# Two graph layers in one kernel: the order of transfers, splittings and matmuls in the first four groups

## What is computed

```python
# layer 0, per graph; 8 heads of 48
q, k, v = x @ wq + bq, x @ wk + bk, x @ wv + bv
scores  = q k^T * 48**-0.5 + adj
ctx     = softmax(scores) @ v
x1      = rmsnorm(x + ctx @ wo + bo) * alpha1 + gamma1
ff      = silu(x1 @ w1 + b1) @ w2 + b2                  # 384 -> 1536 -> 384
x2      = rmsnorm(x1 + ff) * alpha2 + gamma2
x       = layernorm(x + x2)
# layer 1: attention with 12 heads, then layernorm(x + attention(x))
```

## Time and profile before

| | |
|---|---|
| runs | 1919.75, 1922.04, 1927.74 us |
| profiled execution | 1929.19 us, of which 1927.4 us are the span from the first to the last instruction |
| PE busy | 1885.5 us (98%) in 23481 matmuls |
| DVE, ACT, GpSimd busy | 1279.8 (66%), 1084.8 (56%), 496.6 us (26%) |
| DMA | 213.49 MB, 40.2% of 16 engines' span |
| PE in slices of a fortieth | 7 tenths in the first, 8 in the second, 9 or more in all others but the last (7) |
| mean granted TensorE clock | 0.993 of full |

### The profile page before, as it was taken

One profiled execution on the slowest core, in us unless ns is written; L12 is line 12 of the kernel. 1 busy time (PEld: TensorE's weight loads), 2 busy tenths in 40 slices (PEclk: granted clock), 3 DMA queues, 4 the chain that ended last, 5 costly groups with the idle time before them and its releaser, 6 DMA issues.

```text
span 1927.4 us, 60766 instructions
## 1 busy us (share of the span) xinstructions
PE 1885.5 (98%) x23481; PEld 1853.4 (96%) x23481; DVE 1279.8 (66%) x2507; ACT 1084.8 (56%) x2366; POOL 496.6 (26%) x615
## 2 busy tenths in 40 slices
PE   7899999999999999999999999999999999999997
PEld 7899999999999999999999999999999999999997
DVE  6566666666666666666666666654577777777775
ACT  4365555655555654556555565544466666666665
POOL 0121113121122121221211312112134444444443
PEclk9899999999999999999999999999999999999999
DMA  7544444444444434444444344445222333333232
GB/s 190 155 113 108 118 133 109 126 119 109 128 117 118 126 110 128 122 112 123 118 111 136 109 124 116 112 119 122 60 79 84 87 89 90 90 90 90 83 89 68
DMA packets 268686, 213.49 MB, mean 111 GB/s; under 512 B 142816, under 2 KB 251104, under 8 KB 268640
## 3 DMA queue, kind: packets, MB, share of 16 engines
q1 hardware_dynamic: 268640, 212.85, 40.2%
HBM read 120.33 MB, written 79.69 MB: 104 GB/s over the span
## 4 chain that ended last, share of the span: by engine, by line
PE 90%; DMA 2%; SPq 2%; DVE 2%; ACT 1%; issue 1%; POOL 0%; ACTq 0%; POOLq 0%; DVEq 0%
PE a_bank L446 30%; PE a_banks L446 29%; PE b_bank L1444 15%; PE b_banks L1444 5%; PE b_banks L1496 2%; PE a_banks L519 2%; PE b_bank L1515 2%; PE b_banks L1488 2%; PE a_bank L499 2%; SPq L263 1%; DMA xt_raw<-in_xT 0%; PE a_bank L578 0%; DMA ctx_turned<-a_work 0%; DMA a_work<-ctx_turned 0%; DMA xt_raw<-x2T 0%
## 5 line engine op out<-in xcount | busy, mean ns | idle before, releaser
L446 PE MATMUL a_bank<-a_x1t_hi,a_w_hi 128*128 128x256 f32 x1152 | 328.2, 285 | 4.1 <-DVE a_x1t_lo L939 4.1
L446 PE MATMUL a_bank<-a_x1t_lo,a_w_hi 128*128 128x256 f32 x1152 | 325.1, 282 | 0.0
L446 PE MATMUL a_bank<-a_x1t_hi,a_w_lo 128*128 128x256 f32 x1152 | 324.9, 282 | 0.0
L757 ACT ACTIVATE a_work<-a_bank,a_b 128x256 f32<-128x256 f32 x384 | 160.3, 469 | 201.5 <-PE a_bank L446 201.1
L446 PE MATMUL a_banks<-a_w_hi,a_hid_hi 128*128 128x384 f32 x768 | 258.7, 337 | 2.1 <-DVE a_hid_lo L954 2.1
L954 DVE TENSOR_TENSOR a_hid_lo<-a_work,a_hid_hi 128x512 fp32r<-128x512 f32 x192 | 130.7, 694 | 192.8 <-ACT a_hid_hi L762 192.8
L446 PE MATMUL a_banks<-a_w_lo,a_hid_hi 128*128 128x384 f32 x768 | 258.7, 337 | 0.0
L446 PE MATMUL a_banks<-a_w_hi,a_hid_lo 128*128 128x384 f32 x768 | 258.6, 337 | 0.0
L446 PEld LDWEIGHTS a_bank<-a_x1t_hi,a_w_hi 128*128 128x128 f32 x1152 | 218.8, 190 | 6.4 <-DVE a_x1t_lo L939 4.4
L446 PEld LDWEIGHTS a_bank<-a_x1t_lo,a_w_hi 128*128 128x128 f32 x1152 | 221.3, 192 | 0.0
L446 PEld LDWEIGHTS a_bank<-a_x1t_hi,a_w_lo 128*128 128x128 f32 x1152 | 218.0, 189 | 0.0
(11 more groups left out here) (177 smaller groups left out, 5628.2 us busy)
## 6 DMA issues: line engine op xcount, KB each, us to landing
a_work<-in_x SPq DMA_DIRECT2D x64, 384.0 KB, 3.2
p_turned<-a_work SPq DMA_DIRECT2D x256, 64.0 KB, 2.2
a_work<-p_turned SPq DMA_DIRECT2D x32, 512.0 KB, 3.2
xt_raw<-in_xT SPq DMA_DIRECT2D x32, 384.0 KB, 3.9
ctx_turned<-a_work SPq DMA_DIRECT2D x256, 48.0 KB, 1.7
a_work<-ctx_turned SPq DMA_DIRECT2D x32, 384.0 KB, 3.4
x_turned<-a_work SPq DMA_DIRECT2D x256, 48.0 KB, 1.7
a_work<-x_turned SPq DMA_DIRECT2D x32, 384.0 KB, 3.8
```

Source lines behind the costliest of these rows:

```text
L446: r = pe.matmul(out, lhs[a], rhs[b], start=first and n == 0, stop=last and n == 2)
L757: r = act.activation(silu[:, p % 2, s * GROUP:(s + 1) * GROUP], A[p % 3][:, s * GROUP:(s + 1) * GROUP], ACT.Silu, bias=b1[:, m:m + 1])
```

## The change

All in the first layer, in the four `begin` lists and in what they call with group 0 or 1:
- SP: P(0)'s eight stores and the load follow the adjacency of group 1, ahead of w1's second slice. x of group 3 is loaded right behind the constants. w1's third slice moves behind P(1)'s transfers. The stores of x1(0) stand ahead of `load_x(1)`, of `swap_v(2)` and of w2's second half; between its stores and its load stands the first tile of ctx(1), behind the load the second tile, the adjacency of group 3 and ctx(1)'s load.
- Buffers: the blocks of x1(0) are written to `x_bo` in place of `blocks`. `turn_x1(0)` no longer waits for ctx(0)'s stores, `turn_ctx(1)` waits for these in place of x1(0)'s stores, and `load_x(1)` waits for x1(0)'s stores.
- PE: part 0 of `qk(2)` goes ahead of `pv(0)` in place of 30 filling matmuls; the other parts and V follow. 32 filling matmuls stand ahead of `attn_out(0)`; the 45 behind it and the 64 ahead of the feed-forward part go. In the feed-forward part of group 0 `attn_out(1)` moves ahead of `ffn1(0, 3)` and `ffn2(0, 1)`.
- ACT and DVE: the lists follow: `split_x(3)`, `take_pt(1)` and the squares come ahead of w1's third slice and w2; DVE takes ctx(1) ahead of `scale_x1(0)`, with a new wait on the squares; K of group 3, P(2)'s transposition and the low part of x1(0) come ahead of `w1_low(2)`, `w2_low` and V of group 3; x1(1) is made two parts of the hidden layer earlier.

The diff, without the lines that only surround it:

```diff
@@ -46,7 +46,7 @@
...
 N_TURNED = TILES * P // 32
-FILL_FIRST, FILL_LAST, FILL_QK, FILL_OUT = 64, 40, 80, (22, 16)
+FILL_FIRST, FILL_LAST, FILL_QK, FILL_OUT = 32, 40, 80, (22, 16)
@@ -218,6 +218,10 @@
...
+        def x1_blocks(g):
+            return x_bo if isinstance(g, int) and g == 0 else blocks
@@ -233,6 +237,8 @@
...
             def load_x(g):
+                if isinstance(g, int) and g == 1:
+                    sp.wait_ge(x1_stored, 16 * N_TURNED)
                 wait(sp, y1_done, TILES * g)
@@ -273,7 +279,7 @@
...
                 sp.wait_ge(x1_turned, TILES * g + t + 1)
-                store_blocks(blocks, scratch["x1"], t, x1_stored)
+                store_blocks(x1_blocks(g), scratch["x1"], t, x1_stored)
@@ -380,14 +386,14 @@
...
                 load_adj(1)
+                for t in range(TILES):
+                    store_p(0, t)
+                load_pt(0)
                 sp.wait_ge(w_lo, WV + 1)
                 load_w1(1)
-                for t in range(TILES):
-                    store_p(0, t)
-                load_pt(0)
-                load_w1(2)
                 load_x(0)
                 load_consts()
+                load_xt(3)
@@ -398,21 +404,21 @@
...
                 load_pt(1)
-                load_xt(3)
+                load_w1(2)
                 load_w2(range(0, 6))
+                for t in range(TILES):
+                    store_x1(0, t)
+                store_ctx(1, 0)
+                load_x1t(0)
+                store_ctx(1, 1)
+                load_adj(3)
+                load_ctxt(1)
                 load_x(1)
...
                     swap_v(2, t)
-                for t in range(TILES):
-                    store_x1(0, t)
-                load_x1t(0)
                 sp.wait_ge(w1_lo, 2)
                 load_w2(range(6, FC))
-                for t in range(TILES):
-                    store_ctx(1, t)
-                load_adj(3)
-                load_ctxt(1)
                 for t in range(TILES):
@@ -448,9 +454,9 @@
...
-            def qk(g):
+            def qk(g, parts=range(3)):
                 pe.wait_ge(xt_lo, g + 1)
-                for u in range(3):
+                for u in parts:
                     if isinstance(g, int) and g == 0:
@@ -582,9 +588,13 @@
...
                 ffn2(f, 0, new)
+                early = back and isinstance(f, int) and f == 0
+                if early:
+                    for t in range(TILES):
+                        attn_out(f + 1, t, new)
                 ffn1(f, 3, new, back)
                 ffn2(f, 1)
-                if back:
+                if back and not early:
                     for t in range(TILES):
@@ -640,23 +650,21 @@
...
                 scores(1)
-                fill("wq", 30)
+                qk(2, (0,))
                 wait_for_pv(0, True)
...
                     pv(0, t)
-                qkv(2)
+                qk(2, (1, 2))
+                for t in range(TILES):
+                    values(2, t)
+                fill("wq", FILL_FIRST)
                 for t in range(TILES):
                     attn_out(0, t, True)
-                pe.wait_ge(ctx_done, 2)
-                fill("wq", 45)
                 wait_for_pv(1, True)
...
                 qkv(3)
-                pe.wait_ge(ctx_done, TILES * 2)
-                pe.wait_ge(w1_lo, 1)
-                fill("w1", FILL_FIRST)
                 feed_forward(0, True, True)
@@ -855,32 +863,31 @@
...
                     take_q(2, u)
+                split_x(3)
+                ctxt_high(0)
+                for t in range(TILES):
+                    take_pt(1, t)
+                for t in range(TILES):
+                    square(x1, y1_done, ssq1, sq1_done, t + 1, t, ctxt[:, t, :])
+                for t in range(TILES):
+                    keep_v(2, t)
                 w1_high(2)
-                ctxt_high(0)
-                split_x(3)
-                for t in range(TILES):
-                    square(x1, y1_done, ssq1, sq1_done, t + 1, t, ctxt[:, t, :])
-                for t in range(TILES):
-                    take_pt(1, t)
                 w2_high(range(0, 6))
-                for t in range(TILES):
-                    keep_v(2, t)
                 for t in range(TILES):
...
                 act.wait_ge(const_loaded, 16 * N_CONST)
-                for p in range(2):
-                    hidden(0, p)
+                hidden(0, 0)
+                ctxt_high(1)
+                hidden(0, 1)
                 w2_high(range(6, FC))
-                ctxt_high(1)
-                for p in (2, 3):
-                    hidden(0, p)
+                hidden(0, 2)
                 for t in range(TILES):
                     square(x1, y1_done, ssq1, sq1_done, TILES + t + 1, t, ctxt[:, t, :])
-                for p in (4, 5):
+                for p in range(3, FP):
                     hidden(0, p)
@@ -993,7 +1000,9 @@
...
                 dve.wait_ge(ctx_done, 2 * (g + 1))
-                if t == 0:
+                if t == 0 and isinstance(g, int) and g == 1:
+                    dve.wait_ge(ctx_stored, 16 * N_TURNED)
+                elif t == 0:
                     wait(dve, x1_stored, 16 * N_TURNED * g)
@@ -1016,9 +1025,9 @@
...
                 dve.wait_ge(x1_done, TILES * g + t + 1)
-                if t == 0:
+                if t == 0 and not (isinstance(g, int) and g == 0):
                     dve.wait_ge(ctx_stored, 16 * N_TURNED * (g + 1))
-                dve.transpose(blocks[:, t, :], x1[:, t, :]).then_inc(x1_turned, 1)
+                dve.transpose(x1_blocks(g)[:, t, :], x1[:, t, :]).then_inc(x1_turned, 1)
@@ -1191,48 +1200,50 @@
...
                     turn_p(1, t)
+                take_k(2)
+                for t in range(TILES):
+                    take_v(2, t)
+                split_x(3)
                 w1_low(1)
-                take_k(2)
-                for t in range(TILES):
-                    take_v(2, t)
                 turned_low(ctx_t, turned_raw, ctxt_hi, ctxt_lo, 1)
-                split_x(3)
-                w1_low(2)
                 for t in range(TILES):
...
+                dve.wait_ge(sq1_done, TILES)
+                for t in range(TILES):
+                    take_ctx(1, t)
                 dve.wait_ge(const_loaded, 16 * N_CONST)
...
-                for t in range(TILES):
-                    take_ctx(1, t)
                 for t in range(TILES):
...
                     shift(2, t)
+                take_k(3)
+                for t in range(TILES):
+                    turn_p(2, t)
+                turned_low(x1_t, x1t_raw(0), x1t_hi, x1t_lo, 1)
+                w1_low(2)
                 w2_low(range(0, 6))
                 for t in range(TILES):
-                    turn_p(2, t)
-                take_k(3)
-                for t in range(TILES):
                     take_v(3, t)
-                turned_low(x1_t, x1t_raw(0), x1t_hi, x1t_lo, 1)
-                for p in range(2):
+                hidden_low(0, 0)
+                turned_low(ctx_t, turned_raw, ctxt_hi, ctxt_lo, 2)
+                hidden_low(0, 1)
+                w2_low(range(6, FC))
+                hidden_low(0, 2)
+                for t in range(TILES):
+                    take_y1(1, t)
+                scale_x1(1)
+                hidden_low(0, 3)
+                for t in range(TILES):
+                    turn_x1(1, t)
+                for p in (4, 5):
                     hidden_low(0, p)
-                w2_low(range(6, FC))
-                turned_low(ctx_t, turned_raw, ctxt_hi, ctxt_lo, 2)
-                for p in (2, 3):
-                    hidden_low(0, p)
-                for t in range(TILES):
-                    take_y1(1, t)
-                hidden_low(0, 4)
-                scale_x1(1)
-                for t in range(TILES):
-                    turn_x1(1, t)
-                hidden_low(0, 5)
                 for t in range(TILES):
```

More of the change, by code:

```diff
@@ L382, in begin @@
                 load_adj(1)
-                sp.wait_ge(w_lo, WV + 1)
-                load_w1(1)
                 for t in range(TILES):
@@ L387, in begin @@
                 load_pt(0)
-                load_w1(2)
+                sp.wait_ge(w_lo, WV + 1)
+                load_w1(1)
                 load_x(0)
                 load_consts()
+                load_xt(3)
                 for t in range(TILES):
@@ L857, in begin @@
                     take_q(2, u)
-                w1_high(2)
+                split_x(3)
                 ctxt_high(0)
-                split_x(3)
+                for t in range(TILES):
+                    take_pt(1, t)
                 for t in range(TILES):
@@ L864, in begin @@
                 for t in range(TILES):
-                    take_pt(1, t)
+                    keep_v(2, t)
+                w1_high(2)
                 w2_high(range(0, 6))
-                for t in range(TILES):
-                    keep_v(2, t)
                 for t in range(TILES):
@@ L1193, in begin @@
                     turn_p(1, t)
-                w1_low(1)
```

(27 more changed lines are left out.)

## The result

The changed kernel takes **1907.12 us** (median of 6 runs, 1903.66 to 1913.06); the kernel before, run beside it, 1922.22 us (6 runs, 1919.75 to 1927.74). The ratio is 0.9919 with a 95% interval of 0.9906 to 0.9932: 15.1 us less, where 13.3 were forecast. The profiled execution took 1906.83 us, its span 1905.0, against 1927.4 before.

What follows compares the result with a forecast made beforehand. PE's own work was taken to set the middle, so time won in the first four groups ends the kernel earlier. The sum of -13.3 on the profiled 1929.19 gives 1915.9; that execution lies 7.15 above the median, so 1908.7 us, range 1903.0 to 1914.5.

Steps and rivals of the forecast that it cites:

- pv(0): P times V of group 0 on PE: start at 38.95 in place of 40.68, 1.7 us earlier.
- pv(1): P times V of group 1 on PE: start at 59.75 in place of 68.35, 8.6 us earlier.
- x1: Group 0's x1: turn_x1 at 64.4, load at 70.8, low part ready and ffn1 starting at 76.3, 15.3 us earlier.
- The first ffn2: Group 0's first ffn2: start at 84.5 against 97.77, 13.3 us earlier, behind 4.7 us of DVE's low parts.
- From the first ffn2 22.09 us without a hole: First ffn2 to the end of group 0: PE had worked 22.09 us there without a hole.
- I keep it at its old price: Stall of 2.17 us at scores(3), explained by no semaphore, counted as unchanged.
- stalls vanish: Rival: scores(3) unbroken and the loop's first round losing its 3.5 us, -15.5 to -19.0, 1905 us; chance 0.15.
- The clock: New holes before attn_out(0) and ffn1 risk descents of 1.6 to 2.1 us each, falling into slack, 2.1 before ffn2.
- clock on the path: Rival: three ffn1 at reduced clock take 10.7 us, ending at 87.0; 2.5 us lost, 1911.2 us; chance 0.13.
- Late landings: Rival: stores of P, ctx and x1 meet other transfers, 5.4 us lost, -7.9, 1914.1 us; chance 0.14.
- slower: Rival: a stall like the 2.17 us at scores(g) in each of 27 loop rounds, 1967 us; chance 0.03.

Runs made afterwards that it cites:

- p_behind: Changed kernel with P(0)'s stores and load behind w1's second slice again; one profiled execution took 1917.61 us.
- xt_late: Changed kernel with x of group 3 loaded behind P(1) again, ahead of w1's third slice; one profiled execution took 1915.79 us.
- x_later: Changed kernel with only load_x(1) moved, behind V(2)'s swaps and w2's second half; one profiled execution took 1909.39 us.
- after_again: The changed kernel once more, unchanged; one profiled execution took 1916.04 us.
- lows_first: Changed kernel with w1_low(2) and three of the first six w2_low ahead of x1's low part on DVE; one profiled execution took 1904.30 us.
- after: The changed kernel itself, as profiled in the first pair with the kernel before; that execution took 1906.83 us.
- one_buffer: Changed kernel with x1(0)'s blocks back in the buffer of ctx's blocks and the two old waits; one profiled execution took 1915.32 us.
- q_behind: Changed kernel with 30 fillings ahead of pv(0) again and all of qk(2) behind it; one profiled execution took 1921.76 us.
- attn_late: Changed kernel with attn_out(1) back behind ffn2(0, 1); one profiled execution took 1908.59 us.
- combo: Changed kernel with the edits of x_later and lows_first, plus 56 fillings for 32 before attn_out(0) and 30 before ffn1; ratio 0.9935 to the kernel before.

## Why the prediction was right

Total, sign and most of the way were right. Two terms of the sum were not, +2.2 at the first ffn2 and -2.6 behind pv(2); that they cancelled is luck.

- **pv(0)**: 1.7 forecast; the profiled pair has 2.7 and p_behind 2.3 to 3.0. The step counted SP's issue time of one slice only; from p_behind to the change the stores come 2.2 earlier, and a load behind the slice took longer (3.6 to 6.5 us against 3.4 to 3.8). pv(1) comes earlier by the same amount.
- **pv(1)**: 59.75 forecast, 59.60 seen, but for another reason. ACT was done at 58.9; PE was still in `attn_out(0)`, 5.85 us at a granted 0.52, after a hole of 3.16. So the clock took back what the earlier P had given. That the two cancelled is chance too. xt_late bears out the cause of the 8.6: x of group 3.
- **x1**: `turn_x1` 64.37 (64.4), load issued at 71.42 (70.8), ffn1 76.95 (76.3). The four issues of ctx(1) took what they should; x1's eight stores took 4.52 in place of 3.90.
- **The first ffn2**: in the profiled execution this step failed by 2.2 us. "1.75 + 6 x 0.49 = 4.7" was DVE's work taken from a stretch without GpSimd; beside GpSimd's additions it was 6.2 (76.81 to 83.02, w1's slice included). 0.6 came from the later ffn1. Where the additions fell elsewhere, as in x_later, ffn1 to ffn2 took 8.17, and the forecast had 8.2.
- **"From the first ffn2 22.09 us without a hole"**: 86.74 to 108.94 is 22.20. Right.
- **"I keep it at its old price" (scores(3))**: wrong. From pv(2) to ffn1 of group 1 it was 2.76 us (108.94 to 111.70) in place of 5.37 (119.86 to 125.23). Only 1.0 of the 2.6 is the stall that is gone; 1.6 are x1(1), which the forecast had made earlier without giving it a term, since the old stall hid the wait for it. The 2.6 make up for what the first ffn2 had lost: 11.0 + 2.6 = 13.6, and at pv(3) 13.5 were measured. The rival "stalls vanish" had this half right, and wrong in the loop's first round, 41.2 to 44.7 in all kernels.
- **The clock**: 7.74 us for the three ffn1 at 0.82, inside the slack, since DVE was late anyway. In after_again they took 8.54 at 0.73 and ffn2 came straight behind: there the rival "clock on the path" held, but at some 0.4 us (DVE's chain gave 8.17 in x_later), not 2.5. The Trainium skill ("TensorE: Matmul & The Clock Gate", Part 1) has the reduced clock as the default that activity lifts; the rows after the 3 to 4 us holes agree, though not each time: after the hole ahead of `attn_out(0)` its 18 matmuls took, to the end of the last, 3.36 us in lows_first (hole 3.34, granted 1.00), 4.94 in after_again (2.96, 0.65) and 5.92 in the change (3.16, 0.52).
- **Late landings, slower**: neither came. Rounds are as long as before within the spread of executions.

The 15.1 us between the medians and the 13.6 of the steps differ by less than two executions of one kernel do. In the profiled pair (22.4 us of span) 13.0 are there at the loop's second round, 5.7 are round length, and the last 3.6 come mostly around the passage to the second layer. Neither of these two is the change's as far as these runs show: in the repeated pair (8.5 us of span, 15.9 at the loop's second round) the rounds took 5.6 back, and what follows them 1.8.

## What to carry to other kernels

In a start with several chains, look for the wait with the most queued behind it on its engine: here one early transfer of x was worth 9 to 10 us, and the other moves that were undone 0.5 to 5. Before a stall is priced, look for the wait that it hides. Price a DVE step from a stretch in which GpSimd does what it will do in the new place, and price a filling by what it does to the next ready time, not by the clock alone. Before a difference of the profiled pair is explained, run both kernels again.

## What the runs showed of the hardware

- **DVE beside GpSimd.** Four subtractions of two operands in SBUF took 3.60 us (0.55 to 1.37 each) beside GpSimd's additions in three traces (after, one_buffer, q_behind) and 1.96 (0.55 each) where these lay elsewhere. In attn_late they overlapped by 1.0 us and DVE kept its 1.96; there the additions took 2.84 in place of 1.97, so GpSimd was the one that stood. In x_later and combo six such subtractions took 4.54 in place of 2.89 where they met the additions. The Trainium skill ("SBUF — State Buffer", Who interferes with whom) has a lock between the two engines, also for a DVE instruction with two operands in SBUF; the trace agrees. The prediction did not apply it.
- **A stall that is tied to a place in PE's list**, 0.2 to 4.6 us, longer the sooner PE gets there; the places seen lie multiples of some 126 matmuls apart, and not each of them stalls.
- **A load behind a large one.** P(0)'s load of 512 KB reached ACT after 3.4 to 3.8 us where it was issued ahead of w1's slice (ten traces), and after 3.6 to 6.5 where it was issued behind (four).
- **Two lengths of one and the same round**, 40.41 and 40.63, constant within an execution to 0.02 (fourteen traces). The difference sits in matmuls of 256 columns behind scores: one every 0.114 us or every 0.118. No view says what sets it.
